# Where a batch's last attention tiles stand among the first tiles of the MLP: one reordering over four queues

## The chip, the cores and the metric

The kernel runs on one core of a Trainium2 chip. Its time is the device time of one execution, in microseconds; three runs of the kernel before gave 280.09, 280.62 and 283.07 us, median 280.62. The profile is of one further execution.

## The reference, cut to what matters

There are 4 batches of 512 rows of 512 columns, so with tiles of 128 rows 4 tiles a batch and 16 in all. Attention first: with the context of the batch, and `@` a matrix product,

```python
energy = query @ key.T                  # 512 x 512 for each batch
attention = softmax(energy)
x = x + layernorm(x) @ attention.T      # this is called x1 below
```

Then the MLP. Its input v is a layer norm of x1; v also stays as its residual:

```python
v  = bf16(layernorm(x1))
h1 = mx_quant(bf16(layernorm(v) * ln_w + ln_b))      # blocks of 32 share an exponent
h2 = mx_quant(bf16(gelu(bf16(h1 @ mx_quant(W1).T + b1))))   # 512 x 2048 for each batch
x  = x1 + bf16(v + bf16(h2 @ mx_quant(W2).T + b2))
```

`mx_quant` takes the largest magnitude of each block of 32, makes a power of two of it, divides by it, clips, and multiplies again.

## The kernel before, in words

Five engines each run one list of instructions in the order in which it is written; nothing is planned at run time. An instruction that waits for a semaphore holds up all that stands behind it in its list. Batches are numbered 0 to 3, the row tiles of a batch t = 0 to 3. In the MLP the 16 tiles are (m, k), tile i = 2m + k.

**First part.** For b = 0 to 3 the engines compute attention of batch b and quantize a quarter of the weights W1 and W2 with it. TensorE (PE) makes energies and `values(b, t)` (L673, L682, L685): 12 fp16 matmuls and a float32 matmul that adds x, into one of two PSUM banks, t % 2; `values(b, t)` waits until `x_plus(b, t - 2)` has emptied its bank. ScalarE (ACT) makes x1 with `x_plus` (L503), squares it with `x1_square` (L511), makes v with `v_out` (L518), and the sums of v and of its squares with `v_sums` (L526, L529). GpSimd (POOL) turns the sums into factors. VectorE (DVE) quantizes weights (L785 to L838), and makes the second layer norm with `times_w` and `plus_b` (L975, L980), one pair for each row tile, then quantizes a batch of it in seven steps, `h1_amax` to `h1_mult` (L785, L859, L864, L871). `tail_parts(b)` lists this work of batch b in six parts: the four pairs, then amax with three small steps, then over, clip and mult.

**The queue of transposes.** SyncE (SP) issues DMA transposes in the order of its list: xT and pT of the attention, `w1_transpose` and `w2_transpose` of 128x2048 bf16 into w1T and w2T, then `h1_transpose` (128x512, from h1q into h1T, which lies in the tile cxT) and `h2_transpose` (128x2048 bf16, from h2q, which lies in pf, into h2T, which lies in xhl). In the first part `front(b)` issues the transposes of batch b; its last two are `w2_transpose(b - 1)` and `w1_transpose(b)`.

**The hand over.** Behind `front(3)` SP has h1T of tiles 0 and 1, w2T of batch 3, and h1T of tile 2. PE has `values(3, 0)`, waits among others for all of w1T, then runs `product1(0, 0)`, `values(3, 1)`, `product1(0, 1)`, `values(3, 2)`, `values(3, 3)`, `product1(1, 0)`. `product1` (L728, L733) fills the four PSUM banks of y in two halves; ACT empties them in two evictions (L579) and makes gelu of them (L583) into phl. A product1 waits for both evictions of the tile ahead. `product2` (L718 and L743) waits for h2T.

**Second part.** PE alternates product1 of tile i + 3 with product2 of tile i. ACT alternates `y_out` of tile i + 3 (two evictions, gelu) with `z_out` of tile i (L592). DVE has a `slot` for each tile: clip of the tile ahead (L887), amax (L785), power, mult of the tile ahead (L892), scale, inverse, over (L882), with a part of the tail between the small steps. What of batches 2 and 3's second layer norm is left is spread over the slots of tiles 0 to 8. POOL adds the residuals (L441, L447), behind its factors of batch 3.

Of the kernel before, what the change touches and what calls it, by code (L numbers as in the profile page):

```python
# [29 lines left out]
def xattn_ffn_kernel(nc, x, ctx_in, wq, bq, wk, bk, ln_w, ln_b, w1, b1, w2, b2, out):  # L30
    B, L, H = x.shape
# [4 lines left out]
    LT = L // P  # L36
# [19 lines left out]
    with ExitStack() as stack:  # L56
# [161 lines left out]
        def _(sp):  # L218
# [29 lines left out]
            def front(b, ctx=None, later=None):  # L248


                x_transpose(b, 0)
                if ctx is not None:
                    load_ctx(ctx)
                p_transpose(b, 0)
                x_transpose(b, 1)
                p_transpose(b, 1)
                x_transpose(b, 2)
                p_transpose(b, 2)
                p_transpose(b, 3)
                x_transpose(b, 3)  # L260
                if later is not None:
                    load_x(later)
                if b > 0:
                    w2_transpose(b - 1)
                w1_transpose(b)

            def w1_transpose(u):
                wait_alone(sp, w_step[W1], W_STEPS * (u + 1), sp_gate)
                sp.dma_start_transpose(
                    w1T[:, bass.ds(4 * u, 4), :, :].rearrange("p r k f -> p (r k) f"), wquant[:, W1, :])\  # L270
                    .then_inc(w1T_rdy, 16)
# [183 lines left out]
        def _(act):  # L455
# [42 lines left out]
            def x_plus(b, t):  # L498

                if t == 0:  # L500
                    wait_alone(act, mr_rdy, b + 1, act_gate)
                wait_alone(act, pv_ps, b * LT + (t + 1), act_gate)
                act.activation(xs[:, LT * b + t, :], ps_pv[:, t % 2, :], ACT.Identity, bias=mr[:, b, t:t + 1],  # L503
                               scale=1.0 / (XSCALE * PSCALE), accum_out=sums[:, 0, 0, t:t + 1])\
                   .then_inc(x1_rdy, 1)

            def x1_square(b, t):

                if t == 0:
                    wait_alone(act, nm, b + 1, act_gate)  # L510
                act.activation(vs[:, LT * b + t, :], xs[:, LT * b + t, :], ACT.Square,  # L511
                               bias=mean[:, 0, t:t + 1], accum_out=sums[:, 0, 1, t:t + 1]).then_inc(x1_sq, 1)

            def v_out(b, t):

                if t == 0:
                    wait_alone(act, off_rdy, b + 1, act_gate)
                act.activation(vs[:, LT * b + t, :], xs[:, LT * b + t, :], ACT.Identity,  # L518
                               scale=rs[:, 1, t, 1:2], bias=off[:, t:t + 1]).then_inc(v_rdy, 1)

            def v_sums(b, t):

                if t >= 2:
                    act.wait_ge(v_sq, b * LT + (t - 1))
                wait_alone(act, v_rdy, b * LT + (t + 1), act_gate)
                act.activation(squares[:, t % 2, :], vs[:, LT * b + t, :], ACT.Square,  # L526
                               accum_out=sums[:, 1, 1, t:t + 1]).then_inc(v_sq, 1)
                wait_alone(act, v_sq, b * LT + (t + 1), act_gate)
                act.activation(vs[:, LT * b + t, :], vs[:, LT * b + t, :], ACT.Copy,  # L529
                               accum_out=sums[:, 1, 0, t:t + 1]).then_inc(v_sum, 1)  # L530
# [41 lines left out]
                batch(b, b + 1, b + 2, b - 1)  # L572
            batch(B - 2, B - 1, None, B - 3)

            def y_out(m, k):
                i = 2 * m + k
                for g in range(2):
                    act.wait_ge(y_ps, 2 * i + (g + 1))
                    act.activation(ys[:, k, 1024 * g:1024 * g + 1024], ps_y[:, 2 * g:2 * g + 2, :], ACT.Copy)\  # L579
                       .then_inc(y_sb, 1)  # L580
                act.wait_ge(y_sb, 2 * i + 2)
                wait(act, h2_step[k], H_STEPS * (m - 1) + 5)
                act.activation(gs[:, k, :], ys[:, k, :], ACT.Gelu_apprx_tanh).then_inc(g_rdy, 1)  # L583

            def z_out(m, k):
                i = 2 * m + k
# [7 lines left out]

            for t in range(LT):
                v_out(B - 2, t)
            v_sums(B - 2, 0)
            v_sums(B - 2, 1)
            v_sums(B - 2, 2)
            v_sums(B - 2, 3)  # L600
            for t in range(NT):
                act.wait_ge(pT_rdy[t], 16 * B)
            for k in range(2):
                x_plus(B - 1, k)
                y_out(0, k)
            x_plus(B - 1, 2)
            x_plus(B - 1, 3)
            for t in range(LT):
                x1_square(B - 1, t)
            y_out(1, 0)  # L610
            for t in range(LT):
                v_out(B - 1, t)

            def step(m, k):
                if not isinstance(m, int) or 2 * m + k + 3 < T:
                    y_out(*tile(m, k, 3))
                z_out(m, k)

            step(0, 0)
            for t in range(LT):  # L620
                v_sums(B - 1, t)
            step(0, 1)
            with act.Fori(1, T // 2 - 2) as m:
                for k in range(2):
                    step(m, k)
# [6 lines left out]
        def _(pe):  # L632
# [40 lines left out]
            def values(b, t):  # L673

                if t == 0:
                    for n in range(NT):
                        pe.wait_ge(pT_rdy[n], 16 * (b + 1))
                pe.wait_ge(xT_rdy[t], 16 * (b + 1))
                wait(pe, x1_rdy, b * LT + (t - 1))
                pairs = [(a, c, n) for a, c in ((0, 0), (1, 0), (0, 1)) for n in range(NT)]  # L680
                for s, (a, c, n) in enumerate(pairs):
                    pe.matmul(ps_pv[:, t % 2, :], xT[:, t, NT * a + n, :], pTs[b % 2][:, :, NT * c + n, :],  # L682
                              start=(s == 0), stop=False)

                pe.matmul(ps_pv[:, t % 2, :], ident_x[:, :], xs[:, LT * b + t, :],  # L685
                          start=False, stop=True).then_inc(pv_ps, 1)
# [33 lines left out]
            def product1(m, k, z=None):  # L720
                i = 2 * m + k
                pe.wait_ge(h1T_rdy[k], 16 * (m + 1))
                wait(pe, y_sb, 2 * i)
                if z is not None:
                    bias2(*z)
                for c in (1, 2, 3, 0):
                    row = BLOCK * c
                    pe.matmul(ps_y[:, c, :], ones[row:row + 3, :], b1row[row:row + 3, :],  # L728
                              start=True, stop=False)
                for g in range(2):  # L730
                    for c in (2 * g, 2 * g + 1):
                        for t in range(KT):
                            last = pe.matmul(ps_y[:, c, :], h1T[:, k, t, :], w1T[:, 4 * c:4 * c + 4, t, :],  # L733
                                             start=False, stop=(t == KT - 1))
                    last.then_inc(y_ps, 1)
# [10 lines left out]


            values(B - 1, 0)
            pe.wait_ge(c_ones, 1)
            pe.wait_ge(row_b1, 16 * 3 * LT)  # L750
            pe.wait_ge(row_b2, 48)
            pe.wait_ge(w1T_rdy, 16 * B)
            pe.wait_ge(p_exp, T)

            for k in range(2):
                if k > 0:
                    values(B - 1, k)
                product1(0, k)
            values(B - 1, 2)
            values(B - 1, 3)  # L760
            product1(1, 0)

# [20 lines left out]
        def _(dve):  # L783
# [277 lines left out]
            def tail_parts(b):  # L1061

                return [[lambda t=t: times_w(b, t), lambda t=t: plus_b(b, t)] for t in range(LT)] + [
                    [lambda: h1_amax(b), lambda: h1_power(b), lambda: h1_scale(b), lambda: h1_inverse(b)],
                    [lambda: h1_over(b), lambda: h1_clip(b), lambda: h1_mult(b)]]
# [17 lines left out]
            for b in range(3, B):  # L1083
                front(b, b, b - 1, None, b - 3)
                back(b, b, b, b - 2)
            for part in tail_parts(B - 3)[LT:]:
                for part_step in part:
                    part_step()

            def slot(m, k, tail, first=False, last=False):  # L1090


# [19 lines left out]
                    h2_over(m, k)  # L1112


            w_over(W2, B - 1)
            w_clip(W2, B - 1)
            w_mult(W2, B - 1)
            parts = tail_parts(B - 2)
            for part in parts[:LT]:
                for part_step in part:  # L1120
                    part_step()
            dve.wait_ge(w1T_rdy, 16 * B)
            slot(0, 0, parts[LT], True)
            dve.wait_ge(w2T_rdy, 16 * B)
            slot(0, 1, parts[LT + 1])
            slot(1, 0, [])
            parts = tail_parts(B - 1)
            parts = [[], parts[0], parts[1] + parts[2]] + parts[3:]
            for i in range(3, 3 + len(parts)):
                slot(i // 2, i % 2, parts[i - 3])  # L1130
            slot(LT, 1, [])
# [34 lines left out]
```

## Time and profile before

| what | value |
|---|---|
| median of three runs | 280.62 us |
| profiled execution, its own time | 280.04 us |
| profiled execution, span | 278.2 us |
| PE busy | 227.6 us, 82% |
| DVE busy | 244.0 us, 88% |
| ACT busy | 171.3 us, 62% |
| POOL busy | 67.0 us, 24% |
| mean granted clock of PE | 0.935 |

The span runs from the first to the last instruction; the time of the profiled execution is 1.84 us longer than its span. Busy time is a sum over all stages, and the engines are limited by different things in different stages, so the stretch in which the order changes has to be read by itself. That stretch begins at about 120 us, with the last attention tiles, and ends at about 190 us.

### The profile page before, as it was taken

The page shows a single profiled execution, that of the slowest core. Times are in us where ns is not written, and L with a number is a line of the kernel's source. Part 1 is how long each engine was busy: PE and PEld are TensorE (multiplying, and loading weights), DVE is VectorE, ACT ScalarE, POOL GpSimd, SP SyncE. Part 2 cuts the span into 40 slices and gives each one's busy share as a digit, 9 for nine tenths or more (in the row PEclk, how much of TensorE's full clock was granted, in tenths as well). Part 3 has the DMA queues.
Part 4 walks back from the last instruction along what each step waited for, and adds up shares of the span by engine and source line. Part 5 has one row for each costly group of instructions (what it writes and reads, how often), then busy time and mean ns, then how long its engine had stood idle before and what let it go on. Part 6 is the DMA issues. An engine that isn't in the chain of part 4 may idle for free.

```text
span 278.2 us, 3187 instructions
## 1 busy us (share of the span) xinstructions
PE 227.6 (82%) x937; PEld 99.0 (36%) x946; DVE 244.0 (88%) x361; ACT 171.3 (62%) x287; POOL 67.0 (24%) x100
## 2 busy tenths in 40 slices
PE   7766549989976089643599979899999989999993
PEld 7433214434431034211244334344444434444431
DVE  3488998999987999999989998499999999877992
ACT  2267147459994289846586699956665654565510
POOL 2058200022005300052430030512333333333400
PEclk9997968999999669959599999999999999999998
DMA  5978999999999346981440046445354556565673
GB/s 152 387 255 187 250 223 230 283 251 238 231 256 271 76 78 139 240 151 32 84 94 20 13 81 97 94 111 119 73 121 107 132 132 132 132 132 115 145 181 126
DMA packets 103077, 42.92 MB, mean 154 GB/s; under 512 B 93844, under 2 KB 96152, under 8 KB 102552
## 3 DMA queue, kind: packets, MB, share of 16 engines
q1 hardware_dynamic: 100224, 35.93, 58.9%
q10 hardware_dynamic: 2360, 6.83, 8.1%
q0 software_dynamic: 480, 0.02, 0.1%
q8 instruction: 5, 0.08, 0.1%
q14 instruction: 8, 0.07, 0.1%
HBM read 15.48 MB, written 4.19 MB: 71 GB/s over the span
## 4 chain that ended last, share of the span: by engine, by line
DVE 38%; PE 32%; ACT 14%; DMA 8%; issue 4%; POOL 2%; SPq 1%; ACTq 0%; DVEq 0%; POOLq 0%
DVE amax L785 9%; PE ps L743 9%; PE ps L733 8%; PE ps L682 8%; DMA xs<-in_x 4%; DMA xhl<-pf 3%; DVE hq L980 3%; DVE vw L975 3%; DVE pf L892 3%; PE ps L685 2%; DVE w_int L828 2%; DVE stats L939 2%; DVE wquant L882 2%; ACT phl L583 2%; ACT wst L579 2%
## 5 line engine op out<-in xcount | busy, mean ns | idle before, releaser
L733 PE MATMUL ps<-w1T,cxT 128*128 128x512 bf16 x256 | 60.1, 389 | 0.0
L743 PE MATMUL ps<-w2T,xhl 128*128 128x512 bf16 x247 | 56.4, 379 | 1.7 <-DMA xhl<-pf 1.2
L579 ACT ACTIVATE wst<-ps 128x1024 bf16<-128x1024 f32 x32 | 32.4, 1020 | 30.5 <-PE ps L733 30.5
L785 DVE TENSOR_REDUCE amax<-phl 128x64 f32<-128x2048 bf16 x16 | 36.5, 2281 | 8.4 <-ACT phl L583 8.3
L733 PEld LDWEIGHTS ps<-w1T,cxT 128*128 128x128 bf16 x256 | 24.2, 100 | 34.4 <-issue 9.2
L670 PE MATMUL ps<-qkT 128*128 128x512 f32 x32 | 18.5, 684 | 21.4 <-ACT pf L475 17.1
L743 PEld LDWEIGHTS ps<-w2T,xhl 128*128 128x128 bf16 x256 | 24.6, 98 | 31.8 <-DMA xhl<-pf 2.8
L583 ACT ACTIVATE phl<-wst 128x2048 bf16<-128x2048 bf16 x16 | 30.6, 1910 | 1.3
L682 PE MATMUL ps<-pT,xT 128*128 128x512 f16 x96 | 23.9, 403 | 7.7 <-DMA pT<-phl 6.0
L441 POOL TENSOR_TENSOR wst<-wst,vs 128x512 bf16<-128x512 bf16 x12 | 14.8, 1234 | 55.8 <-DVE wquant L887 55.8
L682 PE MATMUL ps<-h1q,xT 128*128 128x512 f16 x96 | 24.8, 414 | 0.0
L785 DVE TENSOR_REDUCE amax<-wst 128x64 f32<-128x2048 f32 x8 | 18.1, 2269 | 5.2 <-DMA wst<-in_L_ffn_W 5.2
L475 ACT ACTIVATE pf<-ps,nmax 128x512 f32<-128x512 f32 x16 | 10.8, 678 | 16.8 <-DVE nmax L949 16.8
L592 ACT ACTIVATE wst<-ps 128x512 bf16<-128x512 f32 x16 | 9.5, 595 | 16.2 <-PE ps L743 15.8
L662 PE MATMUL ps<-cxT,wqkT 128*128 128x512 f32 x32 | 16.2, 655 | 3.4 <-ACT cxT L465 3.4
L882 DVE TENSOR_TENSOR wquant<-phl,mxi 128x2048 int16<-128x2048 bf16 x15 | 18.3, 1223 | 0.3
L828 DVE TENSOR_TENSOR w_int<-wst,mxi 128x2048 int16<-128x2048 f32 x8 | 18.3, 2284 | 0.0
L892 DVE TENSOR_TENSOR pf<-wquant,mxs 128x2048 bf16<-128x2048 int16 x15 | 18.2, 1216 | 0.0
L682 PEld LDWEIGHTS ps<-pT,xT 128*128 128x128 f16 x96 | 9.7, 102 | 23.0 <-issue 14.1
L670 PEld LDWEIGHTS ps<-qkT 128*128 128x128 f32 x32 | 5.7, 204 | 31.0 <-ACT pf L475 20.1
L503 ACT ACTIVATE xs<-ps,mr 128x512 f32<-128x512 f32 x16 | 10.8, 677 | 9.4 <-PE ps L685 9.4
L682 PEld LDWEIGHTS ps<-h1q,xT 128*128 128x128 f16 x96 | 10.2, 106 | 17.4 <-issue 9.5
(81 smaller groups left out, 365.5 us busy)
## 6 DMA issues: line engine op xcount, KB each, us to landing
wst<-in_L_ffn_W ACTq DMA_DIRECT2D x6, 1024.0 KB, 6.1
xs<-in_x SPq DMA_DIRECT2D x4, 1024.0 KB, 8.2
out_x<-wst SPq DMA_DIRECT2D x16, 256.0 KB, 2.9
cx<-in_ctx SPq DMA_DIRECT2D x4, 512.0 KB, 5.6
wst<-in_L_ffn_W SPq DMA_DIRECT2D x2, 1024.0 KB, 9.5
xhl<-pf SPq DMA_TRANSPOSE x17, 4.3
xT<-xhl SPq DMA_TRANSPOSE x16, 4.6
lnw<-in_L_ffn_ln_w ACTq DMA_DIRECT2D x1, 256.0 KB, 7.8
```

The lines of the kernel that those rows point to most:

```text
L441: pool.tensor_tensor(ws[:, k, :], zs[:, k, :], vs[:, i, :], ALU.add).then_inc(zv_rdy, 1)
L579: act.activation(ys[:, k, 1024 * g:1024 * g + 1024], ps_y[:, 2 * g:2 * g + 2, :], ACT.Copy)\
L583: act.activation(gs[:, k, :], ys[:, k, :], ACT.Gelu_apprx_tanh).then_inc(g_rdy, 1)
L662: last = pe.matmul(ps_qk[:, a, :], wqkT[:, a, c, :], cxT[:, c, :], start=(c == 0), stop=(c == CT - 1))
L670: pe.matmul(ps_e[:, t % 2, :], qkT[:, 0, P * t:P * t + P], qkT[:, 1, :], start=True, stop=True).then_inc(e_ps, 1)
L682: pe.matmul(ps_pv[:, t % 2, :], xT[:, t, NT * a + n, :], pTs[b % 2][:, :, NT * c + n, :], start=(s == 0), stop=False)
L733: last = pe.matmul(ps_y[:, c, :], h1T[:, k, t, :], w1T[:, 4 * c:4 * c + 4, t, :], start=False, stop=(t == KT - 1))
L743: last = pe.matmul(ps_z[:, k, :], h2T[:, k, t, :], w2T[:, t, :], start=False, stop=(t == FT - 1))
L785: dve.tensor_reduce(amax[:, a, :], by_block, AX_X, ALU.max, apply_absolute_value=True)\
L828: dve.tensor_tensor(blocks(w_int[:, :]), blocks(wst[:, a, :]), inverse, ALU.mult)\
L882: dve.tensor_tensor(pairs(h2u[:, k, :]), pairs(gs[:, k, :]), per_block(mxi[:, k, :, :]), ALU.mult).then_inc(h2_step[k], 1)
L892: dve.tensor_tensor(pairs(h2q[:, k, :]), pairs(h2u[:, k, :]), per_block(mxs[:, k, :, :]), ALU.mult).then_inc(h2_step[k], 1)
```

## The change

On SP, `front(3)` issues `w1_transpose(3)` before `w2_transpose(2)`; for batches 0 to 2 the order stays. On PE, `values(3, 1)` stands before `product1(0, 0)`, and `values(3, 2)` and `values(3, 3)` each stand behind one product1. On ACT the four `x_plus` of batch 3 stand among the `v_sums` of batch 2 and the evictions and gelus of tiles 0 and 1; two of the four `x1_square` and of the `v_sums` of batch 3 stand behind a later tile. On DVE the pairs of row tiles 2 and 3 of batch 2 and the steps of its quantizing go into the slots of tiles 0, 1 and 2, and the pairs of batch 3 begin one slot later. No instruction is added or taken away.

```diff
@@ SP, front(b, ...)
-                if b > 0:
+                if b < B - 1:
+                    if b > 0:
+                        w2_transpose(b - 1)
+                    w1_transpose(b)
+                else:
+                    w1_transpose(b)
                     w2_transpose(b - 1)
-                w1_transpose(b)
@@ ACT: y_out(m, k) is now y_evict(m, k), then gelu(m, k)
             for t in range(LT):
                 v_out(B - 2, t)
+            x_plus(B - 1, 0)
             v_sums(B - 2, 0)
             v_sums(B - 2, 1)
+            x_plus(B - 1, 1)
             v_sums(B - 2, 2)
             v_sums(B - 2, 3)
+            y_evict(0, 0)
+            x_plus(B - 1, 2)
             for t in range(NT):
                 act.wait_ge(pT_rdy[t], 16 * B)
-            for k in range(2):
-                x_plus(B - 1, k)
-                y_out(0, k)
-            x_plus(B - 1, 2)
+            gelu(0, 0)
+            y_evict(0, 1)
             x_plus(B - 1, 3)
-            for t in range(LT):
-                x1_square(B - 1, t)
+            gelu(0, 1)
+            x1_square(B - 1, 0)
+            x1_square(B - 1, 1)
             y_out(1, 0)
+            x1_square(B - 1, 2)
+            x1_square(B - 1, 3)
...
             step(0, 0)
-            for t in range(LT):
-                v_sums(B - 1, t)
+            v_sums(B - 1, 0)
+            v_sums(B - 1, 1)
             step(0, 1)
+            v_sums(B - 1, 2)
+            v_sums(B - 1, 3)
@@ PE
             values(B - 1, 0)
+            values(B - 1, 1)
...
-            for k in range(2):
-                if k > 0:
-                    values(B - 1, k)
-                product1(0, k)
+            product1(0, 0)
             values(B - 1, 2)
+            product1(0, 1)
             values(B - 1, 3)
             product1(1, 0)
@@ DVE
-            for part in parts[:LT]:
-                for part_step in part:
-                    part_step()
+            for part_step in parts[0] + parts[1]:
+                part_step()
             dve.wait_ge(w1T_rdy, 16 * B)
-            slot(0, 0, parts[LT], True)
+            slot(0, 0, parts[2], True)
             dve.wait_ge(w2T_rdy, 16 * B)
-            slot(0, 1, parts[LT + 1])
-            slot(1, 0, [])
+            slot(0, 1, parts[3] + parts[4])
+            slot(1, 0, parts[5])
             parts = tail_parts(B - 1)
-            parts = [[], parts[0], parts[1] + parts[2]] + parts[3:]
+            parts = [[], [], parts[0], parts[1] + parts[2], parts[3] + parts[4], parts[5]]
             for i in range(3, 3 + len(parts)):
                 slot(i // 2, i % 2, parts[i - 3])
```

## Rows read from the trace of the kernel before

**Rows 1.** The chain of waits that ended last: start us, duration us, what.

```profile
129.90 2.05 DVE amax L785
131.95 2.88 DMA cxT<-h1q
134.96 0.61 PE ps L728 x4
141.18 2.59 PE ps L682 x12
144.62 0.33 PE ps L728 x4
148.51 2.59 PE ps L682 x12
...
222.36 1.22 DVE pf L892
223.81 4.30 DMA xhl<-pf
228.16 3.63 PE ps L743 x16
```

**Rows 2.** DVE in order of time: start, duration, instruction, [idle before <-releaser].

```profile
139.09 1.23 DVE L838 TENSOR_TENSOR wquant<-w_int,mxs 128x2048 bf16<-128x2048 int16 x1
141.53 0.75 DVE L975 SCALAR_TENSOR_TENSOR vw<-vs,mean,lnw 128x512 f32<-128x512 bf16 x1 [1.21 <-POOL rs L365]
144.43 0.75 DVE L975 SCALAR_TENSOR_TENSOR vw<-vs,mean,lnw 128x512 f32<-128x512 bf16 x1
169.87 2.29 DVE L785 TENSOR_REDUCE amax<-phl 128x64 f32<-128x2048 bf16 x1 [0.57 <-ACT phl L583]
179.58 2.29 DVE L785 TENSOR_REDUCE amax<-phl 128x64 f32<-128x2048 bf16 x1 [3.71 <-ACT phl L583]
```

**Rows 3.** The transposes that SP issues, in order of time; the duration is that of the issue.

```profile
65.02 5.04 SPq L275 DMA_TRANSPOSE w2T<-wquant  x1
89.01 2.99 SPq L275 DMA_TRANSPOSE w2T<-wquant  x1
121.18 1.61 SPq L275 DMA_TRANSPOSE w2T<-wquant  x1
129.92 1.92 SPq L269 DMA_TRANSPOSE w1T<-wquant  x1
```

**Rows 4.** Short stretches: PE, PEld, DVE, ACT, POOL busy, granted clock, DMA share, GB/s.

```profile
119.00:119.50 0.50, 0.00 (x0) 0.00 (x0) 0.50 (x1) 0.00 (x0) 0.50 (x1) 0.70 0.00 0
126.00:126.50 0.50, 0.50 (x4) 0.24 (x3) 0.50 (x2) 0.00 (x0) 0.50 (x1) 0.97 0.00 0
132.00:132.50 0.50, 0.00 (x0) 0.00 (x0) 0.43 (x3) 0.47 (x3) 0.00 (x0) 1.00 1.17 214
132.50:133.00 0.50, 0.00 (x0) 0.00 (x0) 0.43 (x3) 0.50 (x3) 0.00 (x0) 0.85 1.16 221
139.50:140.00 0.50, 0.50 (x4) 0.16 (x2) 0.50 (x1) 0.50 (x1) 0.50 (x1) 0.82 0.00 0
```

**Rows 5.** PE in order of time, around its two long idle times.

```profile
115.06 1.02 PE L685 MATMUL ps<-xs,ident_x 128*128 128x512 f32 x2
122.09 4.68 PE L682 MATMUL ps<-pT,xT 128*128 128x512 f16 x12 [6.00 <-DMA pT<-phl]
126.61 1.02 PE L685 MATMUL ps<-xs,ident_x 128*128 128x512 f32 x2
134.96 0.61 PE L728 MATMUL ps<-b1row,ones 3*128 3x512 bf16 x4 [7.33 <-DMA cxT<-h1q]
```

**Rows 6.** ACT in order of time.

```profile
142.25 1.28 ACT L583 ACT_TABLE_LOAD   x1
143.55 1.91 ACT L583 ACTIVATE phl<-wst 128x2048 bf16<-128x2048 bf16 x1
145.37 0.67 ACT L503 ACTIVATE xs<-ps,mr 128x512 f32<-128x512 f32 x1
```

More of the change, by code:

```diff
@@ L573, in _, with y_evict @@
             batch(B - 2, B - 1, None, B - 3)
-            def y_out(m, k):
+            def y_evict(m, k):
                 i = 2 * m + k
@@ L580, in y_out, with gelu @@
                        .then_inc(y_sb, 1)
+            def gelu(m, k):
+                i = 2 * m + k
                 act.wait_ge(y_sb, 2 * i + 2)
@@ L583, in y_out @@
                 act.activation(gs[:, k, :], ys[:, k, :], ACT.Gelu_apprx_tanh).then_inc(g_rdy, 1)
+            def y_out(m, k):
+                y_evict(m, k)
+                gelu(m, k)
             def z_out(m, k):
@@ L1085, in _ @@
                 back(b, b, b, b - 2)
-            for part in tail_parts(B - 3)[LT:]:
-                for part_step in part:
-                    part_step()
             def slot(m, k, tail, first=False, last=False):
@@ L1112, in slot @@
                     h2_over(m, k)
+            for part in tail_parts(B - 3)[LT:]:
+                for part_step in part:
+                    part_step()
             w_over(W2, B - 1)
@@ L1118, in _ @@
             parts = tail_parts(B - 2)
-            for part in parts[:LT]:
-                for part_step in part:
-                    part_step()
+            for part_step in parts[0] + parts[1]:
+                part_step()
             dve.wait_ge(w1T_rdy, 16 * B)
-            slot(0, 0, parts[LT], True)
+            slot(0, 0, parts[2], True)
             dve.wait_ge(w2T_rdy, 16 * B)
-            slot(0, 1, parts[LT + 1])
-            slot(1, 0, [])
+            slot(0, 1, parts[3] + parts[4])
+            slot(1, 0, parts[5])
             parts = tail_parts(B - 1)
-            parts = [[], parts[0], parts[1] + parts[2]] + parts[3:]
+            parts = [[], [], parts[0], parts[1] + parts[2], parts[3] + parts[4], parts[5]]
             for i in range(3, 3 + len(parts)):
```

## The prediction

> **What bounds the kernel now.** I read the chain of waits first, from its end backwards. It says that from 228.16 us PE works without a real pause to the end, and that what started it there was the transpose of tile 8's h2 (issued 223.81), released by DVE's mult of tile 8, which ends at 222.36 + 1.22 = 223.58 [rows 1]. So the end moves by what the end of that one mult moves, as long as PE's product1 work is not later than it. Second I read DVE's own order. Between the end of the last weight step (139.09 + 1.23 = 140.3) and 223.58 it stands still only three times: 1.21 us for POOL's factors of batch 2, 0.57 and 3.71 us for gelus of ACT, together 5.49 [rows 2]. The remaining 83.28 - 5.49 = 77.8 us are work, which the change leaves as it is and only orders anew. That gives one equation for the whole change: **the time moves by DVE's new idle time before mult(8), less 5.49 us.**
>
> PE looks as if it had more to give. It idles 7.33 us before product1(0, 0) [rows 5], and `values(3, 1)` (141.18 to 144.62, 3.44 us) [rows 1] will go into that gap. But from 147 us to 223 us DVE is the slower of the two, so this counts only where it lets DVE start sooner. The same holds for the 3.71 us that DVE waits on ACT: taking it away is worth something only if it is not lost ahead of it.
>
> **When product1(0, 0) starts.** Before, its h1T transpose is issued at 131.95, behind w1T (129.92, which DVE releases), and PE starts at 134.96 [rows 1, 3]. The old list had w2T of batch 2 at 121.18, in an idle queue, at no cost [rows 3]. The new list puts it between w1T and h1T. It is 128x2048 bf16, 524 kB, and the engines move 214 to 221 GB/s while w1T is in flight [rows 4]: 524 kB at 214 is 2.45 us. One queue, one kind of transfer, so I let it go through in order and h1T lands 2.45 us later; PE starts at **137.41**. Lower bound: only the issue is in the way, 1.61 us [rows 3], start 136.6; below that, nothing if the transfers overlap fully. Upper bound: the issue itself stalls as it did twice behind other transposes, 2.99 and 5.04 us [rows 3]; h1T is then issued at 131.95 + 5.04 = 136.99, takes its 2.88 [rows 1], and PE starts near 140.0. DVE's next weight mult wants this w2T too, but only at 139.09, and it has landed by then.
> The Trainium skill (DMA: Bandwidth & Descriptors, Latency and other measured facts) gives 261 GB/s for DMA transposes; w2T would be 2.0 us by that and the start 0.45 us sooner. Nothing below uses it.
>
> **How fast it runs.** PE went idle at 116.08 and the granted clock fell to 0.5 within the half microsecond from 119.0, at 119.2 by its mean of 0.70; it went idle at 127.6 and fell at 132.85 (0.85 over 132.5 to 133.0): 3.1 and 5.2 us after. It came back at 126.0 and at 139.7 (0.82 over 139.5 to 140.0): 3.9 and 4.7 us after work resumed at 122.09 and 134.96 [rows 4, 5]. With values(3, 1) moved up PE goes idle at 127.6 + 3.4 = 131.0, and stays so for 6.4 us. By both pairs the clock has fallen again (134.1 to 136.2) when work resumes at 137.41, and returns after 3.9 to 4.7 us, I take 4.3. A product1 at full clock lasts 148.51 - 144.62 = 3.89 us [rows 1]; at half clock for its first 4.3 us it lasts 3.89 + 2.15. It ends at 137.41 + 6.04 = **143.45**, where it ended at 141.18 before.
>
> **When DVE gets tile 0.** This is the step that costs. Before, ACT ran its table load and gelu(0) right behind the evictions. In the new list x_plus(3, 2) stands before gelu(0), and it waits for values(3, 2), which PE runs behind product1(0, 0). So: 143.45 + 3.44 (values, as above) = 146.89; x_plus with its start 0.8, estimated from 0.67 plus the reading of its accumulator [rows 6], 147.70; table load and gelu 145.37 - 142.25 = 3.12 [rows 6], 150.82. **amax(0) starts at 150.9**. DVE has only four layer-norm instructions to fill the time since 140.3, 144.43 - 141.53 = 2.90 us [rows 2]; the other four, which covered the wait before, are now behind amax(0). New idle: 150.9 - 140.3 - 2.9 = **7.7 us**.
> The factors of batch 2 come up to 1.5 us later on POOL (two x_plus of some 0.76 stand ahead of the last sums); the two layer-norm pairs then end near 146, still under this wait, and cost nothing. If the wait were gone they would cost that 1.5.
>
> **What is given back.** After amax(0) I follow DVE's slots with the old durations: amax(1) is due 6.2 us later (157.1), and gelu(1) ends at 143.45 + 3.45 + 3.89 + 3.45 (values, product1, values) + 0.8 + 1.9 = 156.9. It holds by 0.2. Slot 1 with a layer-norm pair and h1's amax takes 9.9, slot 2 with over, clip and mult 8.9, slot 3 5.9: amax(2), (3), (4) are due at 167.0, 175.9, 181.9. ACT reaches gelu(4) with two v_sums less ahead of it, at 180.4, and gelu(5) at 187.5 against 187.8. So the 0.57, the 3.71 and the 1.21 all disappear: -5.49. Sum: 7.7 - 5.5 = **+2.2 us**. mult(8) ends at 150.9 + 77.8 - 2.9 = 225.8, against 223.6.
> Edits at nothing: moving v_sums(3, 2..3) behind tile 4 makes POOL's factors of batch 3 some 4 us later, covered because their first use on DVE moves a slot later too; POOL's first residual add follows them, and z_out(2) waits for it with under 1 us to spare. If that cover goes, the price is the excess, some tenths.
>
> The profiled execution took 280.04, so 282.2; against the median of 280.62, which lies 0.58 higher, **282.8 us**.
>
> **Rivals.**
> (a) The clock stays up. PE idles 6.4 us instead of 7.33, and if that does not make the clock fall, product1(0, 0) takes 3.89 and ends at 141.3, where it ended before: sum +0.05, 280.6. For it: values(3, 1) shortens the gap. Against it: it fell in a gap of 6.00 [rows 4, 5]. The Trainium skill (TensorE: Matmul & The Clock Gate, What's actually happening) has it that throttled is the default and activity releases it; by that rule filling PE's gap is how this change would pay. Chance 0.15.
> (b) w2T passes beside h1T, and PE starts at 134.96 as before. With the clock as before product1 ends at 141.18, sum -0.1; with the clock up it ends at 138.85, sum -2.4: 278.2 to 280.6. For it: h1T is only a quarter of the size. Against it: the DMA share reads 1.17 while w1T moves [rows 4], which leaves no room. Chance 0.13.
> (c) Slower by over 1%: SP is held by the issue of w2T behind w1T, as at 65.02 [rows 3]. Place: between 131.95 and the issue of h1T(0). Each microsecond of issue above about 2.9 starts PE one later and comes through to mult(8) in full, up to 140.0 - 137.41 = 2.6: 283.4 to 285.4. It decides from an issue of about 3.5 us, since the forecast stands only 0.6 us below the bound. The 0.2 us margins of gelu(1) and gelu(5) work to the same side. Chance 0.27.
>
> **How the numbers follow.** The forecast, 281.6 to 283.4, gets 0.45. The range is to leave out at most the lower end of (b) and the top of (c): 279.3 to 285.2. What this measurement can tell from no change is about 1%, 2.8 us, so 277.8 and 283.4. Faster takes an amax(0) before 145.9, hardly reachable even in (b): 0.07. Slower is (c) and the edge of the forecast: 0.30. Within 1%: 0.63.
>
> **What would show it.** SP: w2T issued at 131.9 right behind w1T, h1T behind it. PE: idle 6.4 before product1(0, 0), its start near 137.4, clock 0.5 under it. ACT: x_plus waiting between the evictions and the table load. DVE: one idle time of over 7 us (in one or two pieces) before the first amax of phl, near 150.9; the old 3.71 gone; mult(8) ending near 225.8. I am wrong if gelu(0) comes before 147, or if DVE idles again before mult(8).

## The result, and the profile after

The changed kernel took 284.5 us (median of 4 runs, 282.92 to 285.66) against 280.85 us of the kernel before (4 runs, 280.09 to 283.07). The ratio is 1.0129, 95% interval 1.0089 to 1.0169: slower by a little over 1%, though the interval reaches below 1%. Forecast were 282.8 us, a ratio of 1.008. The measured time lies inside the range of 279.3 to 285.2 and above the narrower 281.6 to 283.4 that had a chance of 0.45; slower by over 1% had 0.30, within 1% had 0.63. The profiled execution took 284.41 us (span 282.6), 4.37 more than that of before, where 2.2 were forecast.

What the prediction listed under "What would show it" for the stretch from 130 to 152 us came in that order, each entry within 0.6 us. The queue of transposes, in order of time; the duration is that of the issue:

```profile
130.09 1.32 SPq L273 DMA_TRANSPOSE w1T<-wquant  x1
131.46 3.58 SPq L279 DMA_TRANSPOSE w2T<-wquant  x1
135.13 2.52 SPq L293 DMA_TRANSPOSE cxT<-h1q  x2
```

w2T stands between w1T and h1T, and its issue holds SP for 3.58 us where it took 1.61 in the idle queue [rows 3]. h1T is issued 3.18 us later than before [rows 1]. PE around it, with its idle time in brackets:

```profile
129.69 1.02 PE L703 MATMUL ps<-xs,ident_x 128*128 128x512 f32 x2
137.71 0.61 PE L746 MATMUL ps<-b1row,ones 3*128 3x512 bf16 x4 [6.99 <-DMA cxT<-h1q]
138.25 5.54 PE L751 MATMUL ps<-w1T,cxT 128*128 128x512 bf16 x16
143.64 2.75 PE L700 MATMUL ps<-pT,xT 128*128 128x512 f16 x12
```

product1(0, 0) starts at 137.71 (forecast 137.41) and gives way to values at 143.64 (143.45). The clock in single microseconds, columns as in [rows 4]:

```profile
134.00:135.00 1.00, 0.00 (x0) 0.00 (x0) 0.94 (x2) 1.00 (x4) 0.00 (x0) 1.00 1.17 216
135.00:136.00 1.00, 0.00 (x0) 0.00 (x0) 0.99 (x1) 0.97 (x4) 0.00 (x0) 0.68 1.17 216
136.00:137.00 1.00, 0.00 (x0) 0.00 (x0) 1.00 (x2) 0.97 (x4) 0.00 (x0) 0.50 0.87 175
...
141.00:142.00 1.00, 1.00 (x3) 0.29 (x2) 0.00 (x0) 0.12 (x1) 1.00 (x1) 0.50 0.28 58
142.00:143.00 1.00, 1.00 (x6) 0.45 (x5) 0.92 (x2) 0.91 (x1) 0.01 (x1) 0.91 1.14 215
```

It fell near 135.4 and came back near 142.2, 4.5 us after work resumed. From 132 to 136 us the DMA engines moved 207 to 216 GB/s with no pause between w1T and w2T, and in the microsecond from 136, in which w2T ends and h1T follows, still 175. Then ACT, and DVE behind it:

```profile
147.28 0.69 ACT L507 ACTIVATE xs<-ps,mr 128x512 f32<-128x512 f32 x1 [2.42 <-PE ps L703]
148.08 1.28 ACT L590 ACT_TABLE_LOAD   x1
149.38 1.91 ACT L590 ACTIVATE phl<-wst 128x2048 bf16<-128x2048 bf16 x1
```

```profile
142.04 0.75 DVE L992 SCALAR_TENSOR_TENSOR vw<-vs,mean,lnw 128x512 f32<-128x512 bf16 x1 [1.55 <-POOL rs L369]
151.39 2.29 DVE L802 TENSOR_REDUCE amax<-phl 128x64 f32<-128x2048 bf16 x1 [6.36 <-ACT phl L590]
```

x_plus(3, 2) waits 2.42 us for PE, gelu(0) waits behind it, and DVE idles 1.55 + 6.36 = 7.91 us before amax(0) (forecast 7.7; the old 1.21 us for POOL's factors is now the 1.55). The waits of 0.57 and 3.71 us that [rows 2] showed are gone, as forecast. But DVE's mult(8) ends later than forecast. Its row, and four rows from between, in order of time:

```profile
187.18 1.53 DVE L904 TENSOR_SCALAR wquant<-wquant 128x2048 int16<-128x2048 int16 x1
...
190.94 1.18 DVE L810 TENSOR_SCALAR pow<-amax 128x64 uint32<-128x64 uint32 x1
...
196.10 0.69 DVE L904 TENSOR_SCALAR wquant<-wquant 128x2048 int16<-128x2048 int16 x1
...
199.03 0.36 DVE L810 TENSOR_SCALAR pow<-amax 128x64 uint32<-128x64 uint32 x1
...
226.69 1.21 DVE L909 TENSOR_TENSOR pf<-wquant,mxs 128x2048 bf16<-128x2048 int16 x1
```

The same clip takes 1.53 us at 187.18 and 0.69 at 196.10, the same power 1.18 and 0.36 (it takes 0.20 for tiles 0 to 3). Beside the two long ones POOL is at work:

```profile
184.42 2.00 POOL L369 TENSOR_TENSOR rs<-rs,half 128x4 f32<-128x4 f32 x1
186.39 1.76 POOL L445 TENSOR_TENSOR wst<-wst,vs 128x512 bf16<-128x512 bf16 x1
188.23 1.49 POOL L451 TENSOR_TENSOR wst<-xs,wst 128x512 f32<-128x512 f32 x1
189.68 1.15 POOL L445 TENSOR_TENSOR wst<-wst,vs 128x512 bf16<-128x512 bf16 x1
190.91 1.15 POOL L451 TENSOR_TENSOR wst<-xs,wst 128x512 f32<-128x512 f32 x1
```

POOL's instructions are longer there too: an add that takes 1.15 us elsewhere takes 1.76 and 1.49, and the last step of the factors 2.00 us where e4 below has 1.04.

**One yardstick for all kernels.** Up to about 120 us the lists are the same in all of them, yet w1T of batch 3 is issued between 129.3 and 130.6 us in ten of the profiles and at 131.8 to 132.2 in the three others (e3, e7, e9). In these three the granted clock over 45 to 50 us was 0.75 to 0.83, in the ten others 1.00; why it came back later there was not studied. So I measure from that issue. H is the start of product1(0, 0), P the start of the first matmul group behind it, A the first amax of phl, M the end of mult(8), all in us from the issue of w1T; the ratio is to the kernel before, on the same chip, with its 95% interval. It is an estimate of its own and need not equal the quotient of two medians.

| kernel | H | P | A | A to M | M | ratio |
|---|---|---|---|---|---|---|
| before | 5.04 | 11.09 | 17.41 | 76.24 | 93.65 | 1 |
| changed | 7.62 | 13.55 | 21.30 | 76.51 | 97.81 | 1.0129 (1.0089 to 1.0169) |
| e1, SP old | 4.99 | 10.42 | 18.17 | 76.74 | 94.91 | 1.0083 (1.0044 to 1.0122) |
| e2, gelus first | 7.57 | 13.70 | 18.32 | 79.99 | 98.31 | 1.0110 (1.0062 to 1.0158) |
| e3, both | 4.98 | 11.32 | 15.94 | 80.09 | 96.03 | 0.9978 (0.9923 to 1.0033) |
| e4, residuals later | 7.58 | 13.66 | 21.41 | 76.66 | 98.07 | 1.0143 (1.0036 to 1.0250) |
| e5, before, SP new | 7.57 | 13.48 | 18.03 | 78.02 | 96.05 | 1.0079 (1.0043 to 1.0114) |
| e7, sums back | 7.64 | 12.96 | 20.71 | 75.71 | 96.42 | 1.0112 (1.0042 to 1.0182) |
| e8, ACT reordered | 5.02 | 10.42 | 15.04 | 76.66 | 91.70 | 0.9872 (0.9822 to 0.9922) |
| e9, as e8, DVE old | 5.01 | 11.55 | 17.75 | 73.71 | 91.46 | 0.9874 (0.9835 to 0.9913) |
| e10, as e8, SP new | 7.58 | 13.98 | 18.61 | 75.93 | 94.54 | 1.0005 (0.9970 to 1.0039) |
| e11, as e2, evictions early | 7.63 | 13.40 | 18.03 | 76.71 | 94.74 | 1.0031 (1.0000 to 1.0061) |
| e12, as e8, PE old | 5.01 | 11.10 | 15.73 | 78.79 | 94.52 | 1.0008 (0.9980 to 1.0035) |

The ratios leave disturbed executions out: of e3's ten runs, which lie between 278.3 and 284.8 us, four are left, and the profiles of e3 and e9 are of executions that were left out.

H to M are read from one execution of each kernel, so some tenths of a microsecond between two of them carry no weight. From M to the end of the span it is 54.6 to 54.7 us in twelve of the thirteen profiles, so the end did move with the end of mult(8). Only e4 has 55.2; there the clock fell near 224.6 us.

From before to changed M grows by 4.16: 2.58 at H, 3.89 by A, and 0.27 between A and M, where the forecast had the order alone bring A to M to 74.9.

A to M can be taken apart in every profile: it is DVE's idle time in it, what the stretched steps have over their usual length, and the rest, DVE's work. In the changed kernel the stretch is 1.53 - 0.69 and 1.18 - 0.20, together 1.82 us, and there is no idle time. The work then comes to 74.7 to 75.0 us in all ten kernels with DVE's new order, and to 71.7 to 72.0 in the three with the old one. The stretch is 1.7 to 1.9 us in the six kernels in which two of batch 3's v_sums stand behind tile 4. It is 0.6 to 0.8 in e7, e8 and e10, in which all four stand ahead of it. It is nothing in before, e5, e9 and e12, in which DVE waits 1.9 us or more at amax(4) while POOL's first adds begin.

### The profile page after: what moved, and what is told of

It reads as the page before. It is cut to its first block, busy times and chain, and to the rows that moved or that the text cites. A ratio compares the mean times of both kernels' runs of the same rounds, so it can differ in the third digit from the quotient of the medians.

```text
span 282.6 us, 3196 instructions
## 1 busy us (share of the span) xinstructions
PE 228.7 (81%) x946; PEld 99.0 (35%) x946; DVE 245.6 (87%) x361; ACT 171.1 (61%) x287; POOL 66.4 (23%) x100
## 4 chain that ended last, share of the span: by engine, by line
DVE 47%; PE 26%; DMA 9%; ACT 7%; issue 4%; SPq 4%; POOL 2%; ACTq 0%; DVEq 0%; POOLq 0%
DVE amax L802 13%; PE ps L761 9%; PE ps L751 7%; PE ps L700 5%; DVE pf L909 4%; DVE wquant L899 4%; DVE hq L997 4%; DVE vw L992 3%; DMA xhl<-pf 3%; DMA wst<-in_L_ffn_W 3%; DVE wquant L904 3%; SPq L245 2%; DMA h1q<-phl 2%; DVE phl L980 2%; DVE hq L876 2%
## 5 line engine op out<-in xcount | busy, mean ns | idle before, releaser
L761 PE MATMUL ps<-w2T,xhl 128*128 128x512 bf16 x256 | 57.9, 379 | 5.9 <-DMA xhl<-pf 5.9
L688 PE MATMUL ps<-qkT 128*128 128x512 f32 x32 | 19.5, 717 | 22.5 <-ACT pf L479 16.6
L445 POOL TENSOR_TENSOR wst<-wst,vs 128x512 bf16<-128x512 bf16 x12 | 15.4, 1284 | 51.0 <-DVE wquant L904 51.0
L680 PE MATMUL ps<-cxT,wqkT 128*128 128x512 f32 x32 | 14.5, 597 | 2.5 <-ACT cxT L469 2.5
L703 PE MATMUL ps<-xs,ident_x 128*128 128x512 f32 x32 | 16.3, 592 | 0.0
```

What stands on the lines that cost most here:

```text
L445: pool.tensor_tensor(ws[:, k, :], zs[:, k, :], vs[:, i, :], ALU.add).then_inc(zv_rdy, 1)
L688: pe.matmul(ps_e[:, t % 2, :], qkT[:, 0, P * t:P * t + P], qkT[:, 1, :], start=True, stop=True).then_inc(e_ps, 1)
L761: last = pe.matmul(ps_z[:, k, :], h2T[:, k, t, :], w2T[:, t, :], start=False, stop=(t == FT - 1))
```

## The experiments

**e1: SP's part undone.** In `front` of the changed kernel:

```diff
-                if b < B - 1:
-                    if b > 0:
-                        w2_transpose(b - 1)
-                    w1_transpose(b)
-                else:
-                    w1_transpose(b)
-                    w2_transpose(b - 1)
+                if b > 0:
+                    w2_transpose(b - 1)
+                w1_transpose(b)
```

> The changed kernel with one part undone: SP issues w2T of batch 2 before w1T of batch 3 again, as before. My theory: the w2T transpose ahead of h1T costs the start of product1(0, 0) the difference between 137.7 us (changed) and about 135.1. PE is then idle for some 4.4 us only. If the clock still falls and comes back near 139.7, product1(0, 0) ends near 141.3, the first amax of phl starts near 149, and the time is 2.3 us below the changed kernel; if the clock stays up, it ends near 139, amax starts near 146.6 and the time is 4 to 4.7 us below. Rival (the transposes overlap and the start is bound by w1T or by something else): start of product1 stays near 137.7 and the time within 0.5 us of the changed kernel.

H falls by 2.63, M by 2.90. The start of product1 is bound by what stands ahead of h1T in the queue. The ratio moves less than M, from 1.0129 to 1.0083, or 1.3 us, with intervals that overlap; the profiled execution, 281.40 us, is among the fastest of the ten, 281.10 to 284.88. The clock fell all the same:

```profile
135.01 0.47 PE L742 MATMUL ps<-b1row,ones 3*128 3x512 bf16 x4 [4.40 <-DMA cxT<-h1q]
```

```profile
134.00:135.00 1.00, 0.00 (x0) 0.02 (x1) 0.93 (x3) 0.97 (x5) 0.00 (x0) 1.00 0.32 65
135.00:136.00 1.00, 0.99 (x6) 0.39 (x7) 1.00 (x1) 1.00 (x3) 0.00 (x0) 0.60 0.63 128
138.00:139.00 1.00, 1.00 (x5) 0.42 (x4) 0.96 (x2) 0.08 (x1) 0.92 (x2) 0.69 0.00 0
```

After 4.40 us of idle time PE had just resumed, at 135.01, when the granted clock went to 0.5, near 135.2; it was back near 138.6. So product1(0, 0) took 5.43 us from H to P instead of 6.05 before. The clock fell a second time, near 159.1 us, 1.7 us after PE had come out of a gap of 2.10 us, and was back near 162.5; that product1 took 5.31 us instead of 3.63. The changed kernel has the same gap (PE back at 160.57) and its clock stayed up.

**e2: the gelus first.** In ACT's list of the changed kernel:

```diff
             y_evict(0, 0)
-            x_plus(B - 1, 2)
             for t in range(NT):
                 act.wait_ge(pT_rdy[t], 16 * B)
             gelu(0, 0)
+            x_plus(B - 1, 2)
             y_evict(0, 1)
-            x_plus(B - 1, 3)
             gelu(0, 1)
+            x_plus(B - 1, 3)
```

> The changed kernel with ACT's gelu(0) ahead of x_plus(3, 2), and gelu(1) ahead of x_plus(3, 3); SP's new order stays. My theory: gelu(0) waits for a value tile that it does not need. The first amax of phl then starts 3.3 us sooner, near 148.1, but the next amaxes depend on gelu(1) and on PE, so of the 3.3 us about 1.8 come through to DVE's mult of tile 8 and to the end: 1.8 us below the changed kernel. Rival (PE bounds this stretch anyway, because x_plus(3, 2) and (3, 3) come later): amax(0) sooner, mult(8) and the end unchanged within 0.5 us.

A comes 2.98 sooner, about as expected (3.3), but M is 0.50 later: neither theory had that. PE shows why:

```profile
159.58 0.37 PE L736 MATMUL ps<-wqk,ones 3*128 3x512 bf16 x1 [1.21 <-ACT wst L583]
...
170.32 0.58 PE L736 MATMUL ps<-wqk,ones 3*128 3x512 bf16 x1 [3.14 <-ACT wst L583]
170.33 1.00 PE L746 MATMUL ps<-b1row,ones 3*128 3x512 bf16 x4
171.26 6.16 PE L751 MATMUL ps<-w1T,cxT 128*128 128x512 bf16 x16
```

product1 of tile 4 waits 3.14 us for the evictions of tile 3, which stand behind four v_out, which wait for POOL's factors. In that gap the clock falls (0.80 in the microsecond from 169, 0.5 behind it), and the product1 takes 6.16 us instead of 3.63. gelu(4) and gelu(5) come late, and DVE idles 1.76 and 1.67 us at amax(4) and amax(5). The ratio, 1.0110, cannot be told from the changed kernel's.

**e3: e1 and e2 together.**

> Both edits together: SP's old order, and each gelu ahead of the x_plus behind it. If the two costs add, the time is the changed kernel less 2.3 (clock falls) or 4.5 (clock stays) less 1.8: 278.3 to 280.3 us in its profiled execution, which is 0 to 2 us below the kernel before. If they are one and the same cost, it is no better than the better of the two alone.

M is 1.78 below the changed kernel, and 1.12 above e1. A nearly adds up (5.36 sooner together; 3.13 and 2.98 apart, and here product1(0, 0) took 0.9 us longer than in e1, under a clock that came back later), but the same wait of 3.14 us is there with its fall of the clock. Not one and the same cost, but a second one that stands behind both. The profiled execution took 284.49 us where 278.3 to 280.3 were expected; w1T is issued 1.9 us later in it than in the changed kernel's. The ratio, 0.9978, is 1.5% below the changed kernel's, more than this profile's M would give; how much the two edits bring together stays open.

**e4: POOL's residual adds held.** In POOL's `add_residual(i)` of the changed kernel:

```diff
-                pool.wait_ge(h2_step[(i + 3) % 2], H_STEPS * ((i + 3) // 2) + 6)
+                j = i + (4 if i < 2 else 3)
+                pool.wait_ge(h2_step[j % 2], H_STEPS * (j // 2) + 6)
```

> The changed kernel with POOL's residual adds of tiles 0 and 1 each held until the clip of one tile later on DVE. In the changed kernel DVE needs 76.5 us from the first amax of phl to the end of mult(8), where the order alone gives 74.9, and two of its instructions are stretched while POOL adds residuals: the clip of tile 4 takes 1.53 us instead of 0.69, the power of tile 5 takes 1.18 instead of 0.20. Theory: it is POOL's work that stretches them. Held later, these two go back to 0.69 and 0.2 to 0.35, and the end comes up to 1.8 us sooner, less what ACT's z_out of tiles 2 and 3 loses by waiting for the adds (some tenths to 1 us). Rival (they are stretched by something else, or the 1.6 us is waits between small instructions): the stretched instructions stay as they are at their place and the time does not move.

The two instructions at their old place are short again, and two others are long, beside the adds of tile 2, which now follow at once on those of tile 1. DVE, and then POOL, in that stretch:

```profile
187.51 0.69 DVE L905 TENSOR_SCALAR wquant<-wquant 128x2048 int16<-128x2048 int16 x1
188.12 2.28 DVE L803 TENSOR_REDUCE amax<-phl 128x64 f32<-128x2048 bf16 x1
190.43 0.35 DVE L811 TENSOR_SCALAR pow<-amax 128x64 uint32<-128x64 uint32 x1
...
199.11 1.64 DVE L993 SCALAR_TENSOR_TENSOR vw<-vs,mean,lnw 128x512 f32<-128x512 bf16 x1
200.67 1.18 DVE L817 TENSOR_SCALAR mxs<-pow 128x128 bf16<-128x128 f32 x1
```

```profile
196.85 1.16 POOL L452 TENSOR_TENSOR wst<-xs,wst 128x512 f32<-128x512 f32 x1
197.96 2.23 POOL L446 TENSOR_TENSOR wst<-wst,vs 128x512 bf16<-128x512 bf16 x1
200.27 1.49 POOL L452 TENSOR_TENSOR wst<-xs,wst 128x512 f32<-128x512 f32 x1
```

The stretch moved with the adds and kept its size (0.9 + 1.0 us), so A to M did not fall. The theory of the place is borne out, the gain is not: I had moved the collision, not taken it away. The ratio, 1.0143 with an interval of 1.0036 to 1.0250, says nothing on either.

**e5: SP's part alone, in the kernel before.** The lines of e1 the other way round.

> The kernel before with SP's part of the change alone: w1T of batch 3 issued before w2T of batch 2. My theory: this part alone moves the start of product1(0, 0) from 134.96 to about 137.6, and since the gelus, evictions and amaxes behind it all follow from it, it comes through: mult(8) and the end 2.4 to 2.9 us later than before. Rival (it only costs together with the new order on PE and ACT, since before it the layer norms on DVE cover up to 147.3): amax(0) barely later, the end within 0.5 us of before.

H grows by 2.53 and M by 2.40. Here DVE's four layer-norm pairs do cover most of it at A (0.62), but it comes out again at amax(2), which waits 1.84 us for gelu(2) where it had not waited. The waits at amax(3) and amax(4), 0.58 and 3.71, are as before.

**e7: all v_sums of batch 3 ahead of tile 4.** In ACT's list of the changed kernel:

```diff
-            v_sums(B - 1, 0)
-            v_sums(B - 1, 1)
+            for t in range(LT):
+                v_sums(B - 1, t)
             step(0, 1)
-            v_sums(B - 1, 2)
-            v_sums(B - 1, 3)
```

> The changed kernel with one part of ACT undone: all four v_sums of batch 3 stand ahead of the evictions of tile 4, as before. POOL's factors of batch 3 are then ready near 180.5 instead of 186.4, and its residual adds fall into DVE's amaxes again. Theory (POOL's late residual adds stretch DVE's instructions by about 1.8 us): the clip of tile 4 back at 0.69, the power of tile 5 at 0.2 to 0.35; amax(4) waits for a later gelu(4) by 0 to 1 us, so the end is 0.8 to 1.8 us below the changed kernel. Rival (moving v_sums behind tile 4 is what takes away DVE's 3.71 us wait, and its worth is larger than the stretch): the end 1 us later than the changed kernel or more.

A to M falls by 0.80; the other 0.59 of M's 1.39 come from a clock that came back sooner in this run (P at 12.96). DVE did not wait for gelu(4). The clip of tile 4 took 0.69, but the power of tile 4 took 1.01, beside POOL's adds of tile 0: 1.01 us of the stretch of 1.82 went. M is within the 0.8 to 1.8 us expected; the ratio, 1.0112, cannot be told from the changed kernel's. e10 and e11 differ by this one edit as well, and A to M falls there by 0.78, from 76.71 to 75.93.

**e8: a version from all of this.** The changed kernel's PE and DVE, SP's old order, ACT as in e2 and e7, and this:

```diff
             x1_square(B - 1, 0)
             x1_square(B - 1, 1)
-            y_out(1, 0)
+            y_evict(1, 0)
             x1_square(B - 1, 2)
             x1_square(B - 1, 3)
+            gelu(1, 0)
+            y_evict(1, 1)
             for t in range(LT):
                 v_out(B - 1, t)
+            gelu(1, 1)
+            z_out(0, 0)
...
-            step(0, 0)
```

> A version meant to beat both: the changed kernel's PE and DVE, SP's old order, and on ACT each gelu ahead of the x_plus that stands before it, the evictions of tiles 2 and 3 each ahead of work that PE does not wait for (x1_square, v_out), all v_sums of batch 3 ahead of tile 4. Theory: product1(0, 0) starts near 135, amax(0) near 145.3; PE's wait for the evictions of tile 3, 3.14 us in the version with the gelus first, shrinks to nothing, and with it the fall of the clock near 170 us; no DVE instruction is stretched. mult(8) ends near 220 instead of 223.6 and the end is 3 to 3.7 us below the kernel before, near 277. Rival (PE's own work or the h2 transposes bound the stretch once DVE starts sooner): amax(0) near 145.3 but mult(8) at 222 or later, the end within 1.5 us of before.

277.16 us (median of 6, 276.04 to 278.66) against 280.18, ratio 0.9872 (the quotient of the two medians is 0.9892): it beats both kernels. A is at 15.04 and M at 91.70, 1.95 below before. PE's list of idle times over 0.9 us up to mult(8):

```profile
134.35 0.61 PE L743 MATMUL ps<-b1row,ones 3*128 3x512 bf16 x4 [2.83 <-DMA cxT<-h1q]
...
155.78 0.37 PE L733 MATMUL ps<-wqk,ones 3*128 3x512 bf16 x1 [1.21 <-ACT wst L579]
...
168.40 3.63 PE L758 MATMUL ps<-w2T,xhl 128*128 128x512 bf16 x15 [0.93 <-DMA xhl<-pf]
...
173.51 0.38 PE L733 MATMUL ps<-wqk,ones 3*128 3x512 bf16 x1 [1.48 <-ACT wst L579]
```

No gap of 3 us is left behind 134, but the clock fell all the same, near 175.3 us, 1.8 us after PE had come out of the gap of 1.48, and was back near 178.7:

```profile
175.00:176.00 1.00, 1.00 (x5) 0.40 (x4) 0.65 (x1) 0.80 (x2) 0.97 (x1) 0.64 1.16 211
```

That product1 took 5.31 us. mult(8) ended at 221.03, not near 220: one stretched power (0.81) and DVE waits of 0.3 to 0.5 at amax(4), (5) and (6), which I had not expected. The wait at amax(4) ended ahead of that fall, the other two behind it; whether they come from it was not tried.

**e9: e8 with DVE's old order.** DVE's part of the change undone.

> As the version with ACT reordered, with DVE's old order of batch 2's and 3's layer norms. All four layer-norm pairs stand ahead of amax(0) and end near 147.5, so amax(0) starts 2 us later than with DVE's new order, but less work is behind it. Theory: the total on DVE is the same and the two orders come out within 0.5 us of each other; DVE's part of the change is worth something only where gelu(0) comes before 147. Rival (the first h2 tile being 2 us later makes PE wait, and that comes through): 1.5 us or more later than the version with DVE's new order.

A is 2.71 later and M 0.24 sooner; the ratios are 0.9872 and 0.9874. No worth of DVE's part of the change, either way, could be found here; the intervals leave room for about 1%.

**e10: e8 with SP's new order.** The lines of e1 the other way round.

> The fastest version so far (ACT reordered, 277.2 us) with SP's new order put back: w1T of batch 3, then w2T of batch 2, then h1T. Theory: product1(0, 0) starts 2.6 us later and all behind it follows, since nothing in this version covers it: from the issue of w1T to the end of mult(8) 94.1 to 94.9 us instead of 91.7, and the time 2.4 to 3 us higher, near 280. Rival (with PE idle longer and ACT in a better order the delay is absorbed): less than 1 us higher.

H grows by 2.56 and M by 2.84, the ratio from 0.9872 to 1.0005, or 3.7 us, somewhat more than the 2.4 to 3 expected.

**e11: e2 with the evictions of tiles 2 and 3 early.** The diff shown under e8, and nothing else, on e2.

> The version with the gelus first (282.8 us span; PE idle 3.14 us before product1 of tile 4, then 6 us at half clock) with one edit: the evictions of tile 3 stand ahead of the four v_out, those of tile 2 ahead of two x1_square. Theory: PE's 3.14 us wait goes, the clock does not fall near 170, and the gain that putting the gelus first was to give appears: from the issue of w1T to the end of mult(8) 98.3 falls to about 95.5. Rival (the wait and the fall of the clock are beside the path, since DVE has enough to do): 98 stays within 0.7 us.

The wait of 3.14 us is gone, and M falls by 3.57, from 98.31 to 94.74, more than expected: what putting the gelus first was to give was hidden behind ACT's next wait. The ratio goes from 1.0110 to 1.0031, or 2.2 us.

**e12: e8 with PE's old order.** On ACT x_plus(3, 1) moves behind gelu(0, 0) and x_plus(3, 2) behind gelu(0, 1), since their values come later.

```diff
             values(B - 1, 0)
-            values(B - 1, 1)
...
             product1(0, 0)
-            values(B - 1, 2)
+            values(B - 1, 1)
             product1(0, 1)
+            values(B - 1, 2)
             values(B - 1, 3)
```

> The fastest version with PE's old order: values(3, 1) behind product1(0, 0), values(3, 2) and (3, 3) behind product1(0, 1), and the x_plus moved to fit. Theory: values(3, 1) takes 3.45 us of PE out of an idle gap and puts it into the full stretch, so that this much comes back to the end: 3 to 4 us above the fastest version, 280 to 281. Rival (PE is not what bounds the stretch, DVE is, and its work is the same): within 1 us of the fastest version.

M is 2.82 later and the ratio goes from 0.9872 to 1.0008: DVE now waits 0.79 us at amax(0), 1.90 at amax(2) and 1.93 at amax(4). So PE's part of the change, with the x_plus that go with it, is worth 2.8 us, once ACT and SP do not take it away.

## Why the prediction was right, and where it was short

**The equation** (the end moves by DVE's idle time before mult(8)) held but for one term: it took the length of DVE's steps as fixed. With the stretch added it holds in all thirteen profiles, as worked out below the table.

**Start of product1(0, 0).** Right in place and size: 137.71 for 137.41; the delay of H is 2.58 us in the changed kernel, 2.53 in e5 and 2.56 in e10, for the 2.45 that I took as one transfer at 214 GB/s. The trace fits that picture, with the DMA engines full from w1T through w2T. It fits rival (c) in part as well: SP was held for 3.58 us by the issue of w2T. By (c)'s own price, one microsecond for each above 2.9, the start would have been near 138.1; h1T landed 2.5 us after its issue and not 2.88, and that made up for it. Whether the held issue or the full engines set the delay no run separates, and a long issue may only be the sign of full engines. That the result came out so near is partly luck, since I had left the held issue out of the forecast. By the Trainium skill's 261 GB/s for DMA transposes (DMA: Bandwidth & Descriptors, Latency and other measured facts) w2T would take 2.0 us, an estimate; the trace does not agree, the engines moved 207 to 216 GB/s here. e5 and e10 show that the delay comes through whole, 2.40 and 2.84 us at M.

**Clock.** Right: it fell, and product1 took 5.93 us (forecast 6.04). Rival (a) did not come, and by e1 and e8 it would not have come without SP's part either: with gaps of 4.40 and 2.83 us the clock fell all the same. What the shorter gap bought is half a microsecond of product1 (5.43 and 5.40 us in e1 and e8), and both runs lost the clock once more behind a gap of 2.10 or 1.48 us.

**gelu(0) behind x_plus(3, 2).** Right: A at 21.30 for 20.98. e11 shows it to be the second real cost, but only together with the wait behind it; e2 alone would have refuted it.

**What is given back.** Right: the 0.57 and the 3.71 us are gone, and DVE does not idle again between A and M.

**The failed term** is that after amax(0) I follow "DVE's slots with the old durations". From A to M it took 76.51 us and not 74.9. The two stretched instructions alone are 0.84 and 0.98, together 1.82; the other steps came 0.2 shorter than I had added up. I had seen that POOL's factors of batch 3 come some 4 us later, and put them at nothing, or at "some tenths" if their cover went, looking only at who waits for them. What they do is to push POOL's first two pairs of residual adds onto DVE's short steps. Before, the first pair lay in DVE's wait of 3.71 us and in its amax, the second beside an amax and the steps around it, and no step was stretched. e4 moved the stretch with the adds; e7, and e10 against e11, took away somewhat more than half of it. The rest goes only where DVE's wait at amax(4) is kept, so part of what taking that wait away gave was lost again here. That DVE and POOL get in each other's way is shown by place and size; through what is not.

In sum: forecast were 95.88 us from the issue of w1T to M (225.8 - 129.92), measured 97.81. Of the missing 1.93 us, 0.32 had arisen by A and 1.61 between A and M. Five single steps lead from before to the changed kernel, and their effects on M add up to the 4.16: ACT's best order with DVE's new order +0.87 (e12), PE's new order -2.82 (e8), SP's +2.84 (e10), v_sums behind tile 4 +0.20 (e11; +0.78 between A and M, the rest a clock that came back sooner), ACT's gelus and evictions as the change has them +3.07 (changed). Of the parts of the change PE's is worth 2.8 us where the rest lets it through (e12), SP's costs 2.4 to 2.9 (e1, e5, e10), and ACT's, with gelu behind x_plus and the evictions behind x1_square and v_out, 3.1 (e11 against the changed kernel); the evictions without the gelus were not tried, so the 3.1 is not split. DVE's order made no difference in e8 and e9; it was not tried on the changed kernel itself. These prices are of profiles; by the ratios SP's is 1.3 us (e1), 2.2 (e5) and 3.7 (e10), PE's 3.8 and ACT's 2.7.

## What to carry to other kernels

Before a step is moved in an in-order queue, ask what is issued right behind its new place: w2T was free in an idle queue and cost some 2.5 us one place later. On an engine that feeds two others, put first what someone waits for (evictions, then gelu), and put behind it what waits itself (v_out, x_plus): a gain found at one wait shows only when the next wait of the same engine is gone too. A step that is moved may cost more than the wait for it, where it comes to lie beside another engine's short steps.

## What the runs showed of the hardware that was not expected

Beside the residual adds of POOL one or two short VectorE instructions took 0.8 to 1.0 us longer each (0.69 to 1.53, 0.20 to 1.18, 0.75 to 1.64, 0.22 to 1.18), in e8 0.6 (0.20 to 0.81), but its amax of 2.28 us did not. The adds were stretched as well, from 1.15 us to 1.49, 1.76 and, in e4, 2.23.

The granted clock fell after a gap of 4.40 us in e1 and of 2.83 in e8 (0.66 over the microsecond from 134, PE back at 134.35), both at about the moment at which PE resumed. After a gap of 2.10 us at one and the same place it stayed up in the changed kernel and fell in e1 and e7, about 1.5 us after PE had resumed. In e8 it fell 1.8 us after the end of a gap of 1.48, and before kept it after one of 2.17. So the length of a gap alone did not tell in these runs whether the clock would fall.

The issue of the same transpose took 1.61 us in an idle queue and 3.54 to 3.60 right behind another.
